# A transformer layer on eight cores: one-row softmax and norm arithmetic, two x buffers in the attention stage, and wider units in the last matmul stage

## The chip, the cores and the metric

One Trainium2 chip; the same program runs on all 8 NeuronCores, two cores to each of the four batch entries, with no exchange between them. Each core has TensorE (PE, matmuls), VectorE (DVE), ScalarE (ACT), GpSimd (POOL), SyncE (SP) and 16 DMA engines. The metric is the device time in microseconds of the slowest core.

## What is computed

```python
# x: (4, 4096, 2048), float32; 16 query heads, 4 key/value heads of 128
def attn(x):                        # x is layer-normalised
    q, k, v = x @ wq, x @ wk, x @ wv          # split into heads
    q, k = rms_norm(rope(q)), rms_norm(rope(k))
    s = q @ k.T / sqrt(128)                   # causal mask, 4 query heads per k/v head
    return softmax(s) @ v @ wo
def ffn(x):                         # w_gate, w_up: (8192, 2048), w_down: (2048, 8192)
    return (silu(x @ w_gate.T) * (x @ w_up.T)) @ w_down.T
x = x + attn(layernorm(x))
x = x + ffn(layernorm(x))
```

## The kernel before

A core owns 2048 of the 4096 positions of one batch entry, as four blocks ("slots") of 512, and works on everything transposed: features on the 128 partitions, positions along the free axis. The program has five phases, each closed by a barrier of all engines.

1. `ph_const` loads small tables: `selb` (a column of ones), `onesr` (a row of ones, bf16), the mask triangle, the bias `kbb` and the scalars `cst`.
2. `ph_kv` normalises x, projects keys and values for all positions into the resident `kT` and `V`.
3. `ph_slots` goes over the four slots. For each: POOL loads the slot's x as bf16 into `xbq` (L668), waiting for the last DVE instruction of the slot before (`q_v`) and its last statistics matmul (`o1_t`); SP loads the cosine and sine tables `csq`, `snq` (L675, L678); PE sums x over the features into `pR` (L683) and DVE makes the negated mean `negmq` (L689). Then come 16 query heads in a small software pipeline: `q_P` projects (L724, rank-one correction L728), `q_R` does the rope on DVE (L740 to L746), `q_S` squares on ACT, sums on PE and makes the reciprocal root on one row with Ln and Exp (L751 to L761), `q_F` splits this row into two bf16 rows `r_hi`, `r_lo` (L768, L770), broadcasts it to 128 partitions by two bf16 matmuls with `onesr` (L301, L303 in `bcast2`) and multiplies (L775). Attention follows for 8 pairs of heads: scores (L816), Exp on ACT (L843), the sums of the probabilities into one row of `pR` (L857) and probabilities times V into `pY` (L864), for 8, 16, 24 or 32 blocks of 128 keys. At the end of a pair DVE takes the reciprocals of the two rows of sums (L885, L887), splits each into two bf16 rows (L888 to L891), PE broadcasts them with four matmuls (L893 to L900), and DVE copies them out of PSUM and scales `pY` into `yT` (L903 to L908). Then the output projection: 16 steps, each with a block of `wo` on POOL (L929), a block of the residual `xr` on SP (L935), 16 matmuls (L947), the addition (L954), a store of the sum to `scr_out1` (L961) and its copy as bf16 into `xbq` (L966). Last the second layernorm: squares on ACT (L975), sums on PE (L981, L985), the rows by `ln_rows` (L280 to L297), two broadcasts into `pS0`, and multiplication and subtraction over the block on DVE (L999, L1004), stored to `scr_ln2` (L1010).
4. `ph_f1` holds the normalised block of all 2048 positions in SBUF and makes silu(gate) times up, 64 steps of 128 matmuls (L1088, L1101), stored as bf16 in `scr_gated`; beside it the down weights are turned into bf16 in `scr_wd`.
5. `ph_f2` is the down projection. A unit is one block of 512 positions and `DSETW` = 4 blocks of 128 output features, so there are 16 units; their results stand in `pDa` and `pDb` in turn. A unit has 8 steps; a step loads 8 x 128 hidden rows of `scr_gated` into `gld` (L1173) and of `scr_wd` into `wdl` (L1178), double buffered, and does 8 x 4 matmuls (L1199). At the end DVE adds the residual `o1t` (loaded on SP, L1157) for each output block into one of two `ost` tiles (L1211), and SP stores it (L1217).

Every DVE and ACT instruction also waits for the one before it on its own engine. The order on each engine is the order of the program text; each DMA queue is served from the engine that issues it, and a DMA that waits holds back what is behind it on that engine.

Of the kernel before, what the change touches and what calls it, by code (L numbers as in the profile page):

```python
# [50 lines left out]
def host_inputs(cfg, x, wq, wk, wv, wo, wg, wu, wd):  # L51
# [15 lines left out]
    for i in range(128):  # L67
        tri[i, :i] = MASK
    shared["selbuf"] = selbuf
    shared["onesrow"] = onesrow  # L70
    shared["tri"] = tri
    consts = np.array([EPS_LN, EPS_RMS, 1.0 / 128.0, -0.5, SCALE,
                       float(np.log(np.float32(SCALE))), 1.0, 0.0],
# [12 lines left out]
    for c in range(2 * B):  # L86
# [10 lines left out]
        kb = np.zeros((128, NIT), np.float32)  # L97
        u = 0
# [81 lines left out]
def build_program(cfg, dump=()):  # L180
# [9 lines left out]
    DSETW = min(4, DK)  # L190
    NDSET = DK // DSETW
    HGS = min(8, HC)
# [4 lines left out]
    for name, shape, dt in [  # L197
# [6 lines left out]
        ("kbias", [128, NIT], F32), ("tri", [128, 128], BF16),  # L204
        ("selbuf", [128, 32], BF16), ("onesrow", [1, 128], BF16),
        ("consts", [128, 8], F32),
# [17 lines left out]
    if "qy" in dump:  # L224
# [6 lines left out]
              "d_const", "d_xk0", "d_xk1", "d_wkv", "d_cs", "d_cs0", "d_cs1", "d_xq",  # L231
# [9 lines left out]
    with es:  # L241
        selb = sb("selb", [128, 32], BF16)
        onesr = sb("onesr", [1, 128], BF16)
        trib = sb("trib", [128, 128], BF16)
        kbb = sb("kbb", [128, NIT])
# [18 lines left out]
        r_hi = asb0("r_hi", [1, 512], BF16)  # L264
        r_lo = asb0("r_lo", [1, 512], BF16)
        m_hi = asb0("m_hi", [1, 512], BF16)
        m_lo = asb0("m_lo", [1, 512], BF16)
# [11 lines left out]
        def ln_rows(ctx, psA, psB, m_stats, eps_idx):  # L279
# [14 lines left out]
            ctx.op("vector", lambda e: e.tensor_copy(r_hi[:, :], row_r[:, :]))  # L294
            ctx.op("vector", lambda e: e.tensor_sub(r_lo[:, :], row_r[:, :], r_hi[:, :]))
            ctx.op("vector", lambda e: e.tensor_copy(m_hi[:, :], row_mr[:, :]))
            ctx.op("vector", lambda e: e.tensor_sub(m_lo[:, :], row_mr[:, :], m_hi[:, :]))  # L297
            return ctx.c("vm")

        def bcast2(ctx, dst, hi, lo, waits):  # L300
            ctx.op("tensor", lambda e: e.matmul(dst, onesr[0:1, :], hi[0:1, :],  # L301
                                                start=True, stop=False), waits=waits)
            ctx.op("tensor", lambda e: e.matmul(dst, onesr[0:1, :], lo[0:1, :],  # L303
                                                start=False, stop=True), inc="tm")
            return ctx.c("tm")

        def ph_const(ctx):
            ctx.op("sync", lambda e: e.dma_start(out=selb[:, :], in_=dram["selbuf"][:, :]), inc="d_const", n=16)
            ctx.op("sync", lambda e: e.dma_start(out=onesr[:, :], in_=dram["onesrow"][:, :]), inc="d_const", n=16)
# [302 lines left out]
        with ExitStack() as at_es:  # L612
# [10 lines left out]
            xbq = asb("xbq", [128, DK * 512], BF16)  # L623
# [3 lines left out]
            reca = asb("reca", [1, 512])  # L627
            recb = asb("recb", [1, 512])
            ra_hi = asb("ra_hi", [1, 512], BF16)
            ra_lo = asb("ra_lo", [1, 512], BF16)  # L630
            rb_hi = asb("rb_hi", [1, 512], BF16)
            rb_lo = asb("rb_lo", [1, 512], BF16)
# [8 lines left out]
            lnt2 = asb("lnt2", [128, (DK // 8) * 512 if DK >= 8 else 512])  # L641
# [4 lines left out]
            xr0 = asb("xr0", [128, 512])  # L646
            xr1 = asb("xr1", [128, 512])
# [13 lines left out]
            def ph_slots(ctx):  # L661
# [3 lines left out]
                      "qcol_s": 0}  # L665
                for slot in range(NS):
                    uslot = sum(ITERS[:slot])
                    ctx.op("gp", lambda e, slot=slot: e.dma_start(  # L668
                        out=A(xbq, 0, [[DK * 512, 128], [512, DK], [1, 512]]),
                        in_=A(dram["xqT"].tensor, slot * 512,  # L670
                              [[OWN, 128], [128 * OWN, DK], [1, 512]])),
                        waits=[("vm", mk["q_v"]), ("tm", mk["o1_t"])],
                        inc="d_xq", n=16)
# [21 lines left out]
                    def q_P(qc):  # L695
# [22 lines left out]
                        for dk in range(DK):  # L718
                            w = []
                            if dk == 0:  # L720
                                w = [(f"d_wq{buf}", m_wq), ("d_xq", m_xq),
                                     ("vm", mq["ropeM"].get(qc - 2, 0)),
                                     ("sm", mq["exp"].get(qc - 2, 0))]
# [522 lines left out]
```

How the kernel before makes its waits and increments, by code:

```python
    def op(self, engine, fn=None, waits=(), inc=None, n=1, guard=True):  # L129
        waits = [(s, v) for (s, v) in waits if v > 0]
        if engine in ("vector", "scalar") and fn is not None:
            gsem = "vm" if engine == "vector" else "sm"
            if guard and self.cnt[gsem] > 0:
                waits.append((gsem, self.cnt[gsem]))
            if inc is None:
                inc = gsem
        if self.cur == engine:
            for s, v in waits:
                self.eng.wait_ge(self.sems[s], v)
            if fn is not None:
                instr = fn(self.eng)
                if inc is not None:
                    instr.then_inc(self.sems[inc], n)
        if fn is not None and inc is not None:
            self.cnt[inc] += n
```

## Time and profile before

| | |
|---|---|
| median of 5 runs | 7091.7 us (7051.29 to 7437.0) |
| the profiled execution | 7094.07 us |
| its span on the slowest core (core 5) | 7092.5 us |
| spans of the 8 cores | 7016.3 to 7092.5 us |
| PE busy | 5254.0 us (74%) |
| DVE, ACT, POOL busy | 1350.8, 1271.3, 350.2 us |

The profile is of one execution, on its slowest core. PE is the matmul engine, PEld its weight loads, which run beside matmuls; a busy PE isn't one at its peak. In the lists of groups, names stand as output<-inputs without buffer numbers, and "idle before" is the time the engine stood still just before such instructions, with what ended it. PEclk is the share of TensorE's full clock that was granted. SPq and POOLq are the queues of SP and POOL in which DMAs are issued.

### The profile page before, as it was taken

The page shows a single profiled execution, that of the slowest core. Times are in us where ns is not written, and L with a number is a line of the kernel's source. Part 1 is how long each engine was busy: PE and PEld are TensorE (multiplying, and loading weights), DVE is VectorE, ACT ScalarE, POOL GpSimd, SP SyncE. Part 2 cuts the span into 40 slices and gives each one's busy share as a digit, 9 for nine tenths or more (in the row PEclk, how much of TensorE's full clock was granted, in tenths as well). Part 3 has the DMA queues.
Part 4 walks back from the last instruction along what each step waited for, and adds up shares of the span by engine and source line. Part 5 has one row for each costly group of instructions (what it writes and reads, how often), then busy time and mean ns, then how long its engine had stood idle before and what let it go on. Part 6 is the DMA issues. An engine that isn't in the chain of part 4 may idle for free. (4 is left out here: it accounts for less than half of the span.)

```text
span 7092.5 us, 57151 instructions; the slowest of 8 cores (7016.3 to 7092.5 us)
## 1 busy us (share of the span) xinstructions
PE 5254.0 (74%) x21360; PEld 1994.4 (28%) x21360; DVE 1350.8 (19%) x1508; ACT 1271.3 (18%) x1307; POOL 350.2 (5%) x342
## 2 busy tenths in 40 slices
PE   5777765557665776478774999999999866766666
PEld 2222221111121111121121444444444322222222
DVE  1222254244315221241211000000000000000000
ACT  1222223113411443136530000000000000000000
POOL 0000010000001000000000101101010000000000
PEclk8777786767777887678886999999999988888888
DMA  4222160552065103530036666666667566666666
GB/s 64 38 30 35 20 63 6 80 67 21 1 88 69 12 1 48 85 36 1 1 48 120 91 101 91 99 95 92 101 91 100 107 214 205 199 208 210 212 213 210
DMA packets 909244, 632.95 MB, mean 89 GB/s; under 512 B 540338, under 2 KB 847538, under 8 KB 908978
## 3 DMA queue, kind: packets, MB, share of 16 engines
q0 software_dynamic: 574752, 205.54, 27.9%
q1 hardware_dynamic: 334226, 423.75, 19.0%
q8 instruction: 180, 2.95, 0.2%
q14 instruction: 86, 0.70, 0.0%
HBM read 725.70 MB, written 109.05 MB: 118 GB/s over the span
## 5 line engine op out<-in xcount | busy, mean ns | idle before, releaser
L1088 PE MATMUL pG<-ln2T,wgb 128*128 128x512 bf16 x4096 | 896.5, 380 | 68.5 <-DMA wub<-wuT 68.5
L1101 PE MATMUL pU<-ln2T,wub 128*128 128x512 bf16 x4096 | 894.5, 379 | 0.0
L843 ACT ACTIVATE probs<-pS,kbb,rsc 128x1024 bf16<-128x1024 f32 (+3 forms) x640 | 729.8, 1140 | 731.0 <-PE pS L816 549.7
L1199 PE MATMUL pDa<-gld,wdl 128*128 128x512 bf16 x2048 | 484.7, 399 | 237.2 <-DMA wdl<-scr_wd 237.1
L1199 PE MATMUL pDb<-gld,wdl 128*128 128x512 bf16 x2048 | 485.4, 400 | 230.2 <-DMA wdl<-scr_wd 230.2
L1088 PEld LDWEIGHTS pG<-ln2T,wgb 128*128 128x128 bf16 x4096 | 401.8, 98 | 553.3 <-issue 72.1
L1101 PEld LDWEIGHTS pU<-ln2T,wub 128*128 128x128 bf16 x4096 | 400.2, 98 | 483.9
L1113 DVE TENSOR_TENSOR gst<-silo,pU 128x2048 bf16<-128x2048 f32 x64 | 146.4, 2288 | 1674.4 <-PE pU L1101 1674.4
L947 PE MATMUL pY<-lyT,wqb 128*128 128x512 bf16 x1024 | 298.0, 463 | 203.2 <-DMA wqb<-wo 176.3
L857 PE MATMUL pR<-probs,selb 128*1 128x512 bf16 (+3 forms) x1280 | 380.3, 380 | 90.4 <-ACT probs L843 48.9
L1110 ACT ACTIVATE silo<-pG 128x2048 f32<-128x2048 f32 x64 | 120.1, 1877 | 1621.0 <-PE pG L1088 1621.0
L816 PE MATMUL pS<-qT,kT 128*128 128x512 bf16 (+3 forms) x1280 | 394.5, 410 | 6.9 <-DVE qT L775 4.5
L864 PE MATMUL pY<-probs,V 128*128 128x512 bf16 (+3 forms) x1280 | 385.8, 385 | 0.0
L724 PE MATMUL pS<-xbq,wqb 128*128 128x512 bf16 x1024 | 315.2, 477 | 62.8 <-ACT rowr L761 30.2
L1199 PEld LDWEIGHTS pDa<-gld,wdl 128*128 128x128 bf16 x2048 | 205.4, 102 | 516.5 <-issue 306.7
L1199 PEld LDWEIGHTS pDb<-gld,wdl 128*128 128x128 bf16 x2048 | 205.7, 102 | 509.9 <-issue 299.8
L496 PE MATMUL ps_V<-wvb,xb 128*128 128x512 bf16 x768 | 227.6, 463 | 157.1 <-ACT V L509 157.1
L893 PE MATMUL pR<-ra_hi,onesr 1*128 1x512 bf16 x32 | 18.5, 579 | 311.0 <-DVE rb_lo L891 311.0
L826 DVE TENSOR_TENSOR pS<-pS,trib 128x256 f32<-128x256 f32 x128 | 55.4, 433 | 923.8 <-PE pS L816 917.4
L947 PEld LDWEIGHTS pY<-lyT,wqb 128*128 128x128 bf16 x1024 | 115.0, 115 | 387.9 <-issue 316.2
L475 PE MATMUL ps_K<-xb,wkb 128*128 128x512 bf16 x768 | 206.0, 430 | 0.0
L816 PEld LDWEIGHTS pS<-qT,kT 128*128 128x128 bf16 x1280 | 118.3, 105 | 249.4 <-issue 188.0
(132 smaller groups left out, 2980.9 us busy)
## 6 DMA issues: line engine op xcount, KB each, us to landing
gld<-scr_gated SPq DMA_DIRECT2D x128, 1024.0 KB, 6.7
wdl<-scr_wd SPq DMA_DIRECT2D x128, 1024.0 KB, 9.7
wqb<-wq POOLq DMA_DIRECT2D x64, 512.0 KB, 6.8
wqb<-wo POOLq DMA_DIRECT2D x64, 512.0 KB, 9.2
wgb<-wgT POOLq DMA_DIRECT2D x64, 512.0 KB, 11.7
wub<-wuT POOLq DMA_DIRECT2D x64, 512.0 KB, 18.3
wds<-wdT POOLq DMA_DIRECT2D x64, 512.0 KB, 19.6
scr_wd<-wds SPq DMA_DIRECT2D x64, 512.0 KB, 13.4
```

The source lines that it names most:

```text
L475: ctx.op("tensor", lambda e, kc=kc, pi=pi, dk=dk, xb=xb: e.matmul(ps_K[:, pi * 512:(pi + 1) * 512], wkb[:, dk * KD + kc * 128: dk * KD + ( ...
L496: ctx.op("tensor", lambda e, ts=ts, dk=dk, xb=xb: e.matmul(ps_V[:, 0:KD], xb[:, dk * 512 + ts * 128: dk * 512 + ts * 128 + 128], wvb[:, dk ...
L724: ctx.op("tensor", lambda e, qc=qc, dk=dk, qp=qp, buf=buf: e.matmul(qp, wqb[buf][:, dk * 128:(dk + 1) * 128], xbq[:, dk * 512:(dk + 1) * 512],
L816: noff=noff, g2=g2: e.matmul(pS[g2][:, h * 512 + noff: (h + 1) * 512], kT[:, kv * KEXT + pos * 128: kv * KEXT + (pos + 1) * 128], qT[:, (h ...
L843: rcol=rcol: e.activation(A(probs[g2], noff, [[1024, 128], [512, 2], [1, 512 - noff]]), A(pS[g2], noff, [[1024, 128], [512, 2], [1, 512 - ...
L857: it=it: e.matmul(pR[0:1, h * 512 + noff:h * 512 + 512], onescol, probs[g2][:, h * 512 + noff:(h + 1) * 512], start=(it == 0), stop=(it == ...
L864: pos=pos, it=it: e.matmul(pY[:, h * 512 + noff:(h + 1) * 512], V[:, pos * KD + kv * 128: pos * KD + (kv + 1) * 128], probs[g2][:, h * 512 ...
L947: ctx.op("tensor", lambda e, dk=dk, yf=yf, pO=pO, buf=buf: e.matmul(pO, wqb[buf][:, yf * 128:(yf + 1) * 128], yT[:, yf * 512:(yf + 1) * 51 ...
L1088: ctx.op("tensor", lambda e, dk=dk, gi=gi, buf=buf: e.matmul(pG[:, gi * 512:(gi + 1) * 512], wgb[buf][:, dk * 128:(dk + 1) * 128], ln2T[:, ...
L1101: ctx.op("tensor", lambda e, dk=dk, gi=gi, buf=buf: e.matmul(pU[:, gi * 512:(gi + 1) * 512], wub[buf][:, dk * 128:(dk + 1) * 128], ln2T[:, ...
L1113: ctx.op("vector", lambda e, buf=buf: e.tensor_mul(gst[buf][:, :], silo[:, :], pU[:, :]), waits=[("tm", m_u), ("sm", mk["silu_s"]), (f"d_g ...
L1199: pD=pD: e.matmul(pD[:, dki * 512:(dki + 1) * 512], wdl[buf][:, hci * DSW + dki * 128: hci * DSW + dki * 128 + 128], gld[buf][:, hci * 512 ...
```

## The change

- At the end of a head pair the reciprocals are made by ACT as Exp(-Ln(sum)), on one row each. The rows stay float32 and are broadcast by one float32 matmul each with a float32 row of ones, `onesrf`. The splitting into two bf16 rows is gone there, in `q_F` and in `ln_rows`; `bcastF` takes the place of `bcast2`.
- `xbq` has two buffers, and the x of the next slot is loaded on POOL once the query heads of this slot are projected. To make room, `xr0`, `xr1` share the memory of `roq0`, `roq1` (so `xr` waits for the last pair's scaling), `reca`, `recb` that of `row_t`, `row_r`; `lnt2` is half as wide, so that the second layernorm squares and applies in pieces half as wide. The bias table is bf16.
- The sums of the next slot wait only for the layernorm's rows (`pRfree`), no longer for its end.
- In `ph_f2` `DSETW` is 8: 8 units of 8 output blocks, all eight PSUM banks in one tile, `pDb` being `pDa`. `o1t` and `wdl` are loaded on POOL, `gld` on SP.

```diff
@@ build_program
-    DSETW = min(4, DK)
+    DSETW = min(8, DK)
     NDSET = DK // DSETW
+    F2ROT = DSETW <= 4
...
@@ ln_rows
             ctx.op("vector", lambda e: e.tensor_mul(row_mr[:, :], row_m[:, :], row_r[:, :]),
                    waits=[("sm", m_rstd)])
-            ctx.op("vector", lambda e: e.tensor_copy(r_hi[:, :], row_r[:, :]))
-            ctx.op("vector", lambda e: e.tensor_sub(r_lo[:, :], row_r[:, :], r_hi[:, :]))
...
-        def bcast2(ctx, dst, hi, lo, waits):
...
+        def bcastF(ctx, dst, row_ap, waits):
+            ctx.op("tensor", lambda e: e.matmul(dst, onesrf[0:1, :], row_ap,
+                                                start=True, stop=True), waits=waits, inc="tm")
+            return ctx.c("tm")
@@ ph_slots
+                def xq_load(slot):
+                    sb2 = slot % 2
+                    ctx.op("gp", lambda e, slot=slot, sb2=sb2: e.dma_start(
+                        out=A(xbqs[sb2], 0, [[DK * 512, 128], [512, DK], [1, 512]]),
...
+                        waits=[("vm", mk["xbq_v"][sb2]), ("tm", mk["xbq_t"][sb2])],
+                        inc=f"d_xq{sb2}", n=16)
+                xq_load(0)
                 for slot in range(NS):
...
-                            waits=([("d_xq", m_xq), ("vm", mk["q_v"])] if dk == 0 else []),
+                            waits=([m_xq0, ("vm", mk["pRfree"])] if dk == 0 else []),
...
                     m_qT = ctx.c("vm")
+                    if slot + 1 < NS:
+                        xq_load(slot + 1)
@@ end of a head pair
-                            ctx.op("vector", lambda e: e.reciprocal(reca[:, :], pR[0:1, 0:512]),
+                            ctx.op("scalar", lambda e: e.activation(reca[:, :], pR[0:1, 0:512],
+                                                                    AF.Ln),
                                    waits=[("tm", m_av)])
...
+                            ctx.op("scalar", lambda e: e.activation(reca[:, :], reca[:, :],
+                                                                    AF.Exp, scale=CC(7, 1)))
...
@@ output projection and second layernorm
-                            waits=[("vm", mk["xres_v"][buf])], inc=f"d_xr{buf}", n=16)
+                            waits=[("vm", max(mk["xres_v"][buf], mk["yev"])),
+                                   (f"d_xr{buf}", ctx.c(f"d_xr{buf}"))], inc=f"d_xr{buf}", n=16)
...
-                    nb = max(1, (DK // 8) * 2)
+                    nb = 2
...
-                    NQB2 = 8 if DK >= 8 else DK
-                    HB2 = DK // NQB2
+                    NQB2 = DK
+                    HB2 = 1
@@ ph_f2
-                    ctx.op("sync", lambda e, gi=gi, dset=dset, ub=ub: e.dma_start(
+                    ctx.op("gp", lambda e, gi=gi, dset=dset, ub=ub: e.dma_start(
                         out=A(o1t[ub], 0, [[DSETW * 512, 128], [512, DSETW], [1, 512]]),
...
-                        waits=[("vm", mk["ep_v"][ub])], inc=f"d_o1{ub}", n=16)
+                        waits=[("vm", mk["ep_v"][ub if F2ROT else 0])], inc=f"d_o1{ub}", n=16)
...
-                    ub = u % 2
+                    ub = (u % 2) if F2ROT else 0
...
-                        ctx.op("sync", lambda e, dset=dset, hg=hg, buf=buf: e.dma_start(
+                        ctx.op("gp", lambda e, dset=dset, hg=hg, buf=buf: e.dma_start(
                             out=A(wdl[buf], 0, [[HGS * DSW, 128], [DSW, HGS], [1, DSW]]),
...
-                            inc=f"d_wl{buf}", n=16)
+                            waits=[("tm", mk["mm_t"][buf])], inc=f"d_wl{buf}", n=16)
```

How the order of the instructions changes, at three places. First the end of a head pair. Before, on DVE, with the semaphores that each waits for (tm, sm and vm count PE, ACT and DVE):

```order
L885 RECIPROCAL reca<-pR 1x512 [waits tm,vm]
L887 RECIPROCAL recb<-pR 1x512 [waits vm]
L888 CAST ra_hi<-reca 1x512 [waits vm]
L889 TENSOR_TENSOR ra_lo<-reca,ra_hi 1x512 [waits vm]
L890 CAST rb_hi<-recb 1x512 [waits vm]
L891 TENSOR_TENSOR rb_lo<-recb,rb_hi 1x512 [waits vm]
L903 COPY roq<-pR 128x512 [waits tm,vm]
```

Now, at the same place on ACT, after the last Exp of the pair; `row_t` and `row_r` are the memory of `reca` and `recb`:

```order
L844 ACTIVATE probs<-pS,kbb,rsc 128x2x128 [waits tm,vm,sm]
L886 ACTIVATE row_t<-pR 1x512 [waits tm,sm]
L889 ACTIVATE row_t<-row_t,cst 1x512 [waits sm]
L891 ACTIVATE row_r<-pR 1x512 [waits sm]
L893 ACTIVATE row_r<-row_r,cst 1x512 [waits sm]
```

Six DVE instructions have become four on ACT; DVE only copies the broadcast rows.

Second, POOL over the slots, in which its DMAs are issued. Before:

```order
L668 DMA xbq<-xqT 128x16x512 [waits tm,sm,vm]
L697 DMA wqb<-wq 128x16x128 x2
L697 DMA wqb<-wq 128x16x128 [waits tm] x14
L929 DMA wqb<-wo 128x16x128 [waits tm] x16
L668 DMA xbq<-xqT 128x16x512 [waits vm,tm]
L697 DMA wqb<-wq 128x16x128 [waits tm] x16
```

Now:

```order
L661 DMA xbq<-xqT 128x16x512 [waits tm,sm,vm]
L698 DMA wqb<-wq 128x16x128 x2
L698 DMA wqb<-wq 128x16x128 [waits tm] x14
L661 DMA xbq<-xqT 128x16x512
L928 DMA wqb<-wo 128x16x128 [waits tm] x16
L698 DMA wqb<-wq 128x16x128 [waits tm] x16
```

The second slot's x has moved ahead of the first slot's `wo` blocks and waits for nothing; the first `wq` blocks of the second slot have no x load ahead of them.

Third, `ph_f2`, at a boundary between units. Before, on SP:

```order
L1217 DMA outT<-ost 128x512 [waits vm] x4
L1157 DMA o1t<-scr_out 128x4x512 [waits vm]
L1173 DMA gld<-scr_gated 128x8x512 [waits tm]
L1178 DMA wdl<-scr_wd 128x8x512
L1173 DMA gld<-scr_gated 128x8x512 [waits tm]
L1178 DMA wdl<-scr_wd 128x8x512
```

Now there are two queues; on POOL, from the start of the stage:

```order
L1161 DMA o1t<-scr_out 128x8x512 [waits tm,sm,vm]
L1161 DMA o1t<-scr_out 128x8x512
L1182 DMA wdl<-scr_wd 128x8x1024 x2
L1182 DMA wdl<-scr_wd 128x8x1024 [waits tm] x6
L1161 DMA o1t<-scr_out 128x8x512 [waits vm]
L1182 DMA wdl<-scr_wd 128x8x1024 [waits tm] x8
```

On SP the stores of a unit's eight results stand ahead of the next unit's `gld`, and on POOL `o1t`, which waits for the last addition of the unit before, stands ahead of the next unit's `wdl`.

## Rows read from the trace of the kernel before

**Rows 1.** The head of the profile's page.

```profile
span 7092.5 us, 57151 instructions; the slowest of 8 cores (7016.3 to 7092.5 us)
```

**Rows 2.** Busy time by stage: slots, F1, F2; the last columns are clock, DMA share, GB/s.

```profile
916.00:3830.00 2914.00, 1882.40 (x6736) 548.21 (x6736) 951.74 (x1188) 947.78 (x937) 150.97 (x132) 0.77 0.31 40
3876.00:5647.00 1771.00, 1770.22 (x8192) 801.98 (x8192) 144.16 (x63) 121.41 (x65) 177.03 (x186) 1.00 0.66 94
5647.00:7092.00 1445.00, 970.10 (x4096) 411.10 (x4096) 46.58 (x65) 0.00 (x0) 0.00 (x0) 0.85 0.68 210
```

**Rows 3.** The waits: engine and line, releaser: us in total, times, longest.

```profile
PE pR L893 <- DVE rb_lo L891: 311.0, 32, 9.7
...
PE pR L683 <- DMA xbq<-xqT: 161.5, 4, 46.6
```

**Rows 4.** What PE sat idle for before the matmuls of L1199 (us, times).

```profile
  DMA wdl<-scr_wd: 467.4, 88
```

**Rows 5.** Timeline at a pair's end: start, us, engine, line; idle and releaser last.

```profile
1097.50 3.35 DVE L885 RECIPROCAL reca<-pR 1x512 f32<-1x512 f32 x1 [1.86 <-PE pY L864]
...
1107.04 0.58 PE L893 MATMUL pR<-ra_hi,onesr 1*128 1x512 bf16 x1 [9.72 <-DVE rb_lo L891]
...
1109.08 0.69 DVE L903 COPY roq<-pR 128x512 f32<-128x512 f32 x1 [2.18 <-PE pR L900]
```

**Rows 6.** Groups by form: count | busy, mean ns of one | idle before.

```profile
L758 ACT ACTIVATE row_t<-pR,cst 1x512 f32<-1x512 f32 x64 | 49.3, 771 | 44.6 <-PE pR L754 44.6
...
L761 ACT ACTIVATE row_r<-row_t,cst 1x512 f32<-1x512 f32 x32 | 23.1, 722 | 3.0
...
L452 PEld LDWEIGHTS ps_rt<-cst,row_r 1*128 1x128 f32 x96 | 21.3, 322 | 39.5 <-issue 39.5
...
L301 PEld LDWEIGHTS pY<-r_hi,onesr 1*128 1x128 bf16 x64 | 5.8, 91 | 31.6 <-issue 31.6
```

**Rows 7.** Timeline at the boundary between the third and the fourth slot.

```profile
2923.50 1.22 DVE L999 TENSOR_TENSOR lnt<-xbq,pS 128x1024 f32<-128x1024 bf16 x1 [1.40 <-PE pS L303]
...
2943.38 1.22 DVE L1004 TENSOR_TENSOR lyT<-lnt,pS 128x1024 bf16<-128x1024 f32 x1
...
2945.21 1.14 POOL L668 DMA_DIRECT2D xbq<-xqT  x1 [68.42 <-DVE lyT L1004]
...
2968.50 5.68 PE L683 MATMUL pR<-xbq,selb 128*1 128x512 bf16 x16 [44.39 <-DMA xbq<-xqT]
...
2978.30 0.68 DVE L740 TENSOR_TENSOR roq<-pS,csq 64x512 f32<-64x512 f32 x1 [3.27 <-PE pS L728]
```

**Rows 8.** Timeline at a boundary between two units of F2.

```profile
5720.97 15.39 PE L1199 MATMUL pDa<-gld,wdl 128*128 128x512 bf16 x64 [3.54 <-DMA wdl<-scr_wd]
...
5736.60 1.49 DVE L1211 TENSOR_TENSOR ost<-pDa,o1t 128x512 f32<-128x512 f32 x2 [87.11 <-PE pDa L1199]
...
5740.60 1.49 DVE L1211 TENSOR_TENSOR ost<-pDa,o1t 128x512 f32<-128x512 f32 x2 [2.52 <-DMA outT<-ost]
5742.59 0.41 SPq L1157 DMA_DIRECT2D o1t<-scr_out  x1
...
5757.08 16.09 PE L1199 MATMUL pDb<-gld,wdl 128*128 128x512 bf16 x64 [20.73 <-DMA wdl<-scr_wd]
```

**Rows 9.** Busy time in two stretches of loading; clock, DMA share, GB/s last.

```profile
20.00:40.00 20.00, 0.08 (x1) 0.08 (x1) 0.00 (x0) 0.00 (x0) 0.00 (x0) 1.00 1.13 164
5743.00:5757.00 14.00, 0.00 (x0) 0.00 (x0) 0.00 (x0) 0.00 (x0) 0.00 (x0) 0.50 0.96 283
```

**Rows 10.** DMA issues: count, KB each, median us from issue to landing.

```profile
wdl<-scr_wd SPq DMA_DIRECT2D x128, 1024.0 KB, 9.7
...
xb<-xkvT POOLq DMA_DIRECT2D x12, 2048.0 KB, 18.0
...
scr_ln<-lyT SPq DMA_DIRECT2D x4, 2048.0 KB, 11.4
...
csq<-cosq SPq DMA_DIRECT2D x4, 128.0 KB, 12.2
```

More of the change, by code:

```diff
@@ L70, in host_inputs @@
     shared["onesrow"] = onesrow
+    shared["onesrf"] = np.ones((1, 128), np.float32)
     shared["tri"] = tri
     consts = np.array([EPS_LN, EPS_RMS, 1.0 / 128.0, -0.5, SCALE,
-                       float(np.log(np.float32(SCALE))), 1.0, 0.0],
+                       float(np.log(np.float32(SCALE))), 1.0, -1.0],
                       np.float32)
@@ new lines, in ph_slots @@
+                            ctx.op("scalar", lambda e: e.activation(recb[:, :], pR[0:1, 512:1024],
+                                                                    AF.Ln))
+                            ctx.op("scalar", lambda e: e.activation(recb[:, :], recb[:, :],
+                                                                    AF.Exp, scale=CC(7, 1)))
+                            m_rec = ctx.c("sm")
+                            ctx.op("tensor", lambda e: e.matmul(pR[:, 0:512], onesrf[0:1, :], reca[0:1, :],
+                                                                start=True, stop=True),
+                                   waits=[("sm", m_rec)])
@@ L902, in ph_slots @@
+                            ctx.op("tensor", lambda e: e.matmul(pR[:, 512:1024], onesrf[0:1, :], recb[0:1, :],
+                                                                start=True, stop=True), inc="tm")
                             m_rb = ctx.c("tm")
                             ctx.op("vector", lambda e: e.tensor_copy(roq0[:, :], pR[:, 0:512]),
-                                   waits=[("tm", m_rb)])
+                                   waits=[("tm", m_rb), ("d_xr0", ctx.c("d_xr0"))])
                             ctx.op("vector", lambda e: e.tensor_copy(tmpq[:, :], pR[:, 512:1024]))
@@ L1140, in build_program @@
             pDa = f2_es.enter_context(nc.psum_tensor("pDa", [128, DSETW * 512], F32))
-            pDb = f2_es.enter_context(nc.psum_tensor("pDb", [128, DSETW * 512], F32))
+            pDb = (f2_es.enter_context(nc.psum_tensor("pDb", [128, DSETW * 512], F32))
+                   if F2ROT else pDa)
             gld = [gld0, gld1]
```

103 lines of the change are left out of this document (40 added, 63 removed).

## The prediction

> **What bounds the kernel now.** I began with the span and its three large stages. The slowest core spans 7092.5 us [rows 1]; the profiled execution took 7094.07 us, 1.6 us more, and the median of the five runs is 7091.7, so a sum made against the profiled execution can be read against the median. By stages [rows 2]: the slots (attention) take 2914 us with PE busy 1882; the first feed-forward stage (F1) 1771 us with PE busy all of it at full clock; the second (F2) 1445 us with PE busy 970 at a mean granted clock of 0.85. F1 is untouched by the edit, so whatever is won or lost lies in the slots and in F2.
>
> Then the waits. In the slots PE stands 311.0 us, 32 times 9.7, before the broadcast of the softmax denominators, for a chain of six DVE instructions, and 161.5 us, 4 times, for the block of x of the next slot [rows 3]. In F2 it stands 467.4 us in 88 waits for wdl [rows 4]. I count 16 of these as long (17.5 to 22.0 us, 322 us together): the first of the stage and one at each of the 15 boundaries between units. The other 72 lie inside units, 145 us in all.
>
> Four changes matter: a shorter chain at the end of a head pair, the early load of x, F2 in 8 units instead of 16, and the small passes of the second layernorm.
>
> **1. End of a head pair (32 times).** Today DVE begins the reciprocals at 1097.50, PE gets its operand at 1107.04 and DVE reads the broadcast at 1109.08 [rows 5]: 9.5 us of rows, then 2.0 us of PE. Now ACT does Ln, Exp, Ln, Exp on one row each, at 771 and 722 ns [rows 6], so 3.0 us, plus three gaps and a hand-over of about 0.1 us each: 3.4 us. That removes 6.1 us. ACT has nothing else then: its next Exp needs the next pair's scores, which stand behind the broadcast on PE. Ln and Exp already follow each other 64 times in the slots with no table load between them, so I charge none.
>
> The broadcast changes from four bf16 matmuls to two float32 ones. No float32 matmul of 512 columns is in the trace. The nearest row is the float32 weight load of 128 columns, 322 ns, against 91 ns for the same load in bf16 [rows 6]: a factor of 3.5. The bf16 matmuls start 0.43 us apart at the half clock, so one float32 matmul is 0.43 us if the type costs nothing and 1.5 us at 3.5 times. Two of them are 0.9 to 3.0 us against 1.7 today; I take the 3.5, the row for the same data type. At the half clock this costs 1.3 us; if PE, idle for 3.7 us instead of 9.7, is still at its full clock, it costs nothing. In F2 a wait of 3.54 us is followed by 64 matmuls in 15.39 us [rows 8] where F1's rate (1771 us for 8192, 0.216 us each) gives 13.8, so part of them ran at half. I therefore lean to the cold price: 6.1 - 1.1 = 5.0 us a pair, **-160 us** (ends: 4.4 and 6.9 us a pair, -140 to -220).
>
> The Trainium skill (FP8 and Floating Point Precision, TensorE Precision Notes) says that true FP32 takes four passes through the array. By that the two matmuls would be 3.4 us at the half clock, 0.4 more than by the row, and this part -150.
>
> The same float32 broadcast serves each query head (64 times) in place of two casts on DVE and two bf16 matmuls. The casts ran beside the square on ACT, so nothing is won; the longer matmul costs 0.32 us at the full clock where DVE is what PE waits for, nothing where PE waits for ACT's Exp anyway. I take **+12 us** (0 to +40).
>
> **2. Slot boundaries (3 times).** DVE ends the layernorm with the row of 2943.38, POOL issues xbq at 2945.21, PE starts its sums at 2968.50, and the first rope of the next slot is at 2978.30 [rows 7]: 33.7 us from end to rope. With two xbq buffers the load runs during attention; PE can do the sums and the first projection while DVE still normalises, and only the mean's row (0.7 us), one matmul and the rope remain. What is late next is the cosine table: its load is still issued when the layernorm ends, on SP behind the 2 MB store of the normalised block. It lands after 12.2 us today and the store after 11.4 [rows 10], both sharing the DMA engines with the xbq load that is gone now; 2 MB at 283 GB/s [rows 9] are 7.4 us, and with both tables behind I take 10 us. So 33.7 becomes 10: -24 each, **-71 us** (ends: 13 us and 2 us, -62 to -95).
>
> **3. The second layernorm (4 times).** Four casts on DVE go (2.6 us), the float32 broadcast adds 0.6 before the first apply and 0.8 before the second. The applies go from 16 of 1.22 us, 1.33 us apart [rows 7], to 32 half as wide; a DVE pass of 512 columns takes 0.69 us [rows 5], with 0.1 between two, so 25.3 us against 21.2. The squares go from 4 wide steps to 8 narrow ones that alternate with PE, +1. Net +4 a slot, **+16 us** (0 to +30). The first residual block xr can no longer be loaded ahead, since it shares roq: +1 a slot, **+4 us**, mostly beside PE's 16 matmuls.
>
> **4. F2.** A unit now has 8 output blocks, so 8 units of 512 matmuls. A step is 64 matmuls, 13.8 us at F1's rate, and needs 1 MB of gld on SP and 2 MB of wdl on POOL, together 3.15 million bytes; it was 2.1 million per 6.9 us. At 283 GB/s [rows 9] that is 11.1 us, and about 2 us of latency makes 13. So the waits inside units nearly vanish: 145 to 10, **-135 us**.
> The half clock after waits goes with them. 4096 matmuls at 0.216 are 885 us; with the 467 of waits that leaves 93 of the 1445, of which I put 13 to the start and end of the stage and 80 to matmuls at half the clock. Eight restarts at 2 us and a few more are 20: **-60 us**.
> The boundaries are fewer and longer. pDb is now pDa, so the next unit may not start before the last add. The adds go in pairs of 1.49 us, the second pair 4.0 us after the first, held by the out stores [rows 8]. Four pairs end at about 13 us instead of 5.5. Only then does POOL issue o1t (2 MB) and wdl, and SP gld. Before wdl has landed 4.2 million bytes go through POOL's queue and up to 2.1 through SP's: 6.3 million at 283 GB/s are 22 us. Before, 14 us did for 3.96 million in just that stretch [rows 8, 9]. 13 + 22 + 2 = 37 us, seven times: 259 against 15 times 20.0 = 300, **-41 us**.
> At the stage's start two o1t loads of 2 MB stand ahead of wdl: +10. The tail has four more adds: +7.
> F2 in all: -135 - 60 - 41 + 17 = **-219 us**.
> That the software queue moves 2 KB pieces as fast as SP's does is the soft point. For it: at the start of the program, with POOL's loads alone, the queue wrote 164 GB/s of bf16 [rows 9], read as twice as much float32. Against it: a 2 MB xb load takes 18.0 us from issue to landing, where wdl on SP took 9.7 for 1 MB [rows 10]. If wdl took those 18.0, a step would be 4 us over, which is +202 on 48 steps. I take the first, since xb reads 4 MB. Range of F2: -20 to -260.
>
> The Trainium skill (DMA: Bandwidth & Descriptors, Issuing engine by pattern) sends simple loads to Sync and calls that path generally faster; this change does the reverse. Its section Issuing engines are not separate DMA queues says all of them run on the same 16 engines and only issue time is saved. By the first rule the second rival below is what to expect, by the latter the forecast.
>
> **Sum.** -160 + 12 - 71 + 16 + 4 - 219 = -418; 7094 - 418 = 6676, and I say **6676 us**.
>
> **Rivals.**
> A. *F2 becomes bound by the software queue.* Steps of 17 instead of 13.8 us, because 2 MB through POOL take near to xb's 18.0. That is 3.2 x 48 = +154, and each boundary (two loads in that queue) +6: in all +196, 6872 us.
> B. *The slots give half.* The float32 broadcast is slower than 3.5 times and the tables hold each slot: 3.2 us a pair is won instead of 5.0, 12 us a slot instead of 24, and each query head pays 0.6: 58 + 36 + 26 = +120, 6796 us. For it: nothing in the trace shows such a matmul.
> C. *Better than forecast.* PE stays at full clock through the pair ends (6.3 us each, -42) and the boundary loads run at 350 GB/s (4 us less, -28): 6606 us.
> D. *Slower than before.* Place: the wait of PE for wdl at each step of F2. If 2 MB on POOL's queue take 18.0 us alone and gld's 1 MB is served beside it (another 3.5), a step is 21.5 us: 7.7 x 48 = +370; two such loads at each boundary +13 x 7, +15 at the start: +476, 7152 us. It decides from a step of 20.5 us on, since each us of step costs 48 plus 14 at the boundaries. Against it: xb reads twice wdl's bytes.
> E. *The change doesn't do what it says:* the early x load waits for a release behind it. The order shows it on POOL ahead of the wo loads with nothing to wait for but the slot before last, so I give this almost nothing: +71, 6747 us.
>
> **How the numbers follow.** Forecast 0.60, A 0.15, B 0.12, C 0.08, D 0.03, E 0.02. 6560 to 6880 holds the forecast with its bounds, A, B, C and E; what is left out is D, an A that is worse than priced and a mixture of A and B. A measurement tells about 1% (71 us) from no change: faster by more 0.95, within 0.02, slower 0.03; only D and something near it come to no gain.
>
> **What would show it.** ACT with four rows between a pair's last matmul and the broadcast, PE's wait there near 3.6 us instead of 9.7; the float32 matmul near 0.75 or 1.5 us. xbq gone from PE's waits in three of four slots, and the table's load as the releaser of the first rope. F2's stretch near 1226 us, 7 waits near 37 us, almost none inside units. I am wrong if PE waits for wdl inside units by more than 3 us a step, or if a boundary is over 45 us, or if the pair's end is not shortened by at least 4 us.

## The result, and the profile after

In some executions of either kernel the cores of one die or of both are granted a lower clock and the time is longer, so all times and ratios below, medians apart, are of executions without that, and the profile of after is read on cores 0 to 3, which had the usual clock in it, mostly on core 1, the slowest of them. Before took 7051 to 7092 us and after 6676.04, 6684.59 and 6704.94 us: a ratio of **0.9452, 95% interval 0.9389 to 0.9516**. Of the 7091.7 us of before that is 6703 us. The forecast of 6676 us is a ratio of 0.941. The medians over all executions are 7330.31 us before (ten) and 6983.38 us after (six); the latter lies above the forecast range of 6560 to 6880 us.

Core 1 after (cores view: span, mean granted clock):

```profile
core 1: 6682.1 us, clock 0.860
```

The same three stages as in [rows 2], slots, F1 and F2:

```profile
916.00:3667.00 2751.00, 1996.75 (x6736) 585.43 (x6736) 597.73 (x916) 1037.07 (x1083) 150.68 (x132) 0.79 0.34 43
3712.00:5484.00 1772.00, 1771.20 (x8192) 802.17 (x8192) 144.14 (x63) 121.43 (x65) 177.03 (x186) 1.00 0.62 94
5484.00:6683.00 1199.00, 903.67 (x4096) 404.03 (x4096) 46.57 (x65) 0.00 (x0) 63.46 (x72) 0.88 0.57 197
```

The slots lose 163 us, F2 246, F1 nothing: about 410 us, all where the prediction looked. DVE's busy time in the slots falls from 952 to 598 us. PE's rises from 1882 to 1997 us; the rows of the broadcasts make up some 80 of these 115 us (140 us in bf16 before, 220 in float32 after).

The waits of PE after (us in total, times, longest), against [rows 3, 4]:

```profile
PE pDa L1203 <- DMA wdl<-scr_wd: 252.6, 10, 37.7
...
PE pR L896 <- ACT row_r L893: 102.1, 32, 3.2
...
PE pS L729 <- DVE negmq L690: 48.9, 3, 16.5
...
PE pDa L1203 <- DMA gld<-scr_gated: 26.5, 1, 26.5
...
PE pR L684 <- DMA xbq<-xqT: 22.2, 1, 22.2
```

At each pair's end PE now waits 3.2 us instead of 9.7. The wait for xbq is there once instead of four times. In F2 the rows for wdl and gld together are 11 waits and 279 us where 88 and 467 stood. The row for negmq is no new loss: those three waits of 16 us are PE, done early with the sums, standing while DVE still normalises, and what follows them is shown below.

A pair's end after, answering to [rows 5]:

```profile
1102.48 0.29 PE L865 MATMUL pY<-probs,V 128*128 128x128 bf16 x2
1102.92 0.59 ACT L886 ACTIVATE row_t<-pR 1x512 f32<-1x512 f32 x1 [0.79 <-PE pY L865]
1103.60 0.72 ACT L889 ACTIVATE row_t<-row_t,cst 1x512 f32<-1x512 f32 x1
1104.41 0.59 ACT L891 ACTIVATE row_r<-pR 1x512 f32<-1x512 f32 x1
1105.09 0.72 ACT L893 ACTIVATE row_r<-row_r,cst 1x512 f32<-1x512 f32 x1
...
1105.96 2.04 PE L896 MATMUL pR<-row_t,onesrf_s 1*128 1x512 f32 x2 [3.19 <-ACT row_r L893]
...
1107.80 1.91 PE L899 MATMUL pR<-row_r,onesrf_s 1*128 1x512 f32 x2
...
1109.63 1.89 PE L817 MATMUL pS<-qT,kT 128*128 128x512 bf16 x4
1109.88 0.69 DVE L902 COPY roq<-pR 128x512 f32<-128x512 f32 x1 [8.80 <-PE pR L899]
```

ACT's four rows stand one behind another (3.0 us from the first to PE's start), then PE needs 3.7 us from 1105.96 to the next scores at 1109.63 for two float32 matmuls, 1.84 us each; the profile shows each as two instructions. The granted clock from 1105.9 to 1109.7 is 0.50, and the bf16 matmuls behind take 0.47 us each: PE is at its half clock. From PE's last matmul to DVE's copy 12.0 us have become 7.4.

The boundary between the third and the fourth slot, answering to [rows 7]:

```profile
2826.17 0.69 DVE L1004 TENSOR_TENSOR lyT<-lnt,pS 128x512 bf16<-128x512 f32 x1
2826.93 0.37 SPq L1010 DMA_DIRECT2D scr_ln<-lyT  x1
...
2827.39 1.96 SPq L676 DMA_DIRECT2D csq<-cosq  x1
2827.90 0.58 PE L729 MATMUL pS<-negmq,qcolsb 1*128 1x512 bf16 x1 [16.25 <-DVE negmq L690]
...
2840.10 0.68 DVE L741 TENSOR_TENSOR roq<-pS,csq 64x512 f32<-64x512 f32 x1 [12.45 <-DMA snq<-sinq]
```

The projection is ready at 2828.5, but the rope stands 12.45 us for the sine table, issued behind the 2 MB store. From the end of the last apply to the rope are 13.2 us where 33.7 were.

The first boundary of F2, answering to [rows 8]:

```profile
5626.63 2.54 PE L1203 MATMUL pDa<-gld,wdl 128*128 128x512 bf16 x11
5629.41 1.49 DVE L1216 TENSOR_TENSOR ost<-pDa,o1t 128x512 f32<-128x512 f32 x2 [142.98 <-PE pDa L1203]
...
5634.16 0.69 DVE L1216 TENSOR_TENSOR ost<-pDa,o1t 128x512 f32<-128x512 f32 x1 [3.26 <-DMA outT<-ost]
...
5645.32 0.69 DVE L1216 TENSOR_TENSOR ost<-pDa,o1t 128x512 f32<-128x512 f32 x1 [0.94 <-DMA outT<-ost]
5646.51 1.10 SPq L1177 DMA_DIRECT2D gld<-scr_gated  x2
5646.55 0.88 POOL L1161 DMA_DIRECT2D o1t<-scr_out  x1 [43.59 <-DVE ost L1216]
5647.43 1.76 POOL L1182 DMA_DIRECT2D wdl<-scr_wd  x2
5666.87 1.44 PE L1203 MATMUL pDa<-gld,wdl 128*128 128x512 bf16 x3 [37.70 <-DMA wdl<-scr_wd]
```

It falls into two halves: 17 us until the last add has gone (5629.2 to 5646.5), the adds after the first two held by the out stores, then 20 us for the loads, none of which is issued before. This is the longest of core 1's first six boundaries: from first to last add they take 13.2 to 16.6 us (14.4 on average); on cores 0, 2 and 3 they take 10.6 to 14.0 us. The DMA issues of core 1 (count, KB each, median us to landing), against 9.7 us for 1 MB on SP [rows 10]:

```profile
wdl<-scr_wd POOLq DMA_DIRECT2D x64, 2048.0 KB, 11.9
```

### The profile page after: what moved, and what is told of

The parts are those of the page before. It is cut to its first block and busy times, and to the rows that moved or that the text cites. A ratio compares the mean times of both kernels' runs of the same rounds, so it can differ in the third digit from the quotient of the medians.

```text
span 6814.2 us, 56736 instructions; the slowest of 8 cores (6644.6 to 6814.2 us)
## 1 busy us (share of the span) xinstructions
PE 5464.8 (80%) x21360; PEld 2061.8 (30%) x21360; DVE 996.9 (15%) x1236; ACT 1358.0 (20%) x1451; POOL 413.2 (6%) x414
## 5 line engine op out<-in xcount | busy, mean ns | idle before, releaser
L1203 PE MATMUL pDa<-gld,wdl 128*128 128x512 bf16 x4096 | 1052.2, 429 | 253.3 <-DMA wdl<-scr_wd 229.2
L1203 PEld LDWEIGHTS pDa<-gld,wdl 128*128 128x128 bf16 x4096 | 439.1, 107 | 866.3 <-issue 770.0
L725 PE MATMUL pS<-xbq,wqb 128*128 128x512 bf16 x1024 | 321.7, 484 | 41.7 <-ACT row_r L763 20.4
L1216 DVE TENSOR_TENSOR ost<-pDa,o1t 128x512 f32<-128x512 f32 x64 | 44.3, 692 | 1270.1 <-PE pDa L1203 1216.3
L725 PEld LDWEIGHTS pS<-xbq,wqb 128*128 128x128 bf16 x1024 | 117.2, 119 | 254.0 <-issue 198.8
L928 POOL DMA_DIRECT2D wqb<-wo x64 | 73.1, 1141 | 1852.0 <-PE pY L947 1785.9
## 6 DMA issues: line engine op xcount, KB each, us to landing
scr_wd<-wds SPq DMA_DIRECT2D x64, 512.0 KB, 10.6
```

What stands on the lines that cost most here:

```text
L725: ctx.op("tensor", lambda e, qc=qc, dk=dk, qp=qp, buf=buf: e.matmul(qp, wqb[buf][:, dk * 128:(dk + 1) * 128], xbq[:, dk * 512:(dk + 1) * 512],
L1203: pD=pD: e.matmul(pD[:, dki * 512:(dki + 1) * 512], wdl[buf][:, hci * DSW + dki * 128: hci * DSW + dki * 128 + 128], gld[buf][:, hci * 512 ...
```

## Experiments

There are nine. After took 6684 us (the middle of its three), before 7053 to 7116 us beside these runs. e3, e4, e5, e6 and e9 rest on one execution each, so a difference of some 20 us in their whole time (after's own three spread over 29) is weak; what is read from marks inside the traces is firmer.

**e1, F2's edits alone on the kernel before.**

```diff
-    DSETW = min(4, DK)
+    DSETW = min(8, DK)
...
-            pDb = f2_es.enter_context(nc.psum_tensor("pDb", ...))
+            pDb = (f2_es.enter_context(...) if F2ROT else pDa)
...
-                        ctx.op("sync", ... wdl[buf] ...
+                        ctx.op("gp", ... wdl[buf] ...
```

> The kernel before with the new ph_f2 alone (8 units of 8 output blocks, o1t and wdl on POOL). Theory 1 (the forecast's mechanism: the gain of F2 is its own and comes from fewer steps' waits, and the slots' gain is separate): F2 takes 1199 us as in the changed kernel against 1445, the slots stay at 2914, so 7092 - 246 = 6846 us, ratio 0.965. Theory 2 (the F2 gain leans on something in the slots, or the two gains overlap): F2 above 1230 us, ratio above 0.97.

Measured: 6837.36 and 6845.66 us, with 8 long waits of 265 us and 0.3 us of short ones in F2, as in after. F2's part is worth 228 us by itself against the two runs of before beside it (7052.77 and 7085.35) and 250 against 7091.7; what is left to after's 6684, some 158 us, is the slots' part, near to the 163 that the slots' stretch lost.

**e2, o1t and wdl on SP's queue**, after otherwise.

```diff
-                    ctx.op("gp", ... o1t[ub] ...
+                    ctx.op("sync", ... o1t[ub] ...
...
-                        ctx.op("gp", ... wdl[buf] ...
+                        ctx.op("sync", ... wdl[buf] ...
```

> The changed kernel with o1t and wdl issued on SP again, DSETW still 8. Theory 1 (the width is what counts: all queues feed the same 16 DMA engines and 3 MB per step fit into 13.8 us either way): F2 stays within 15 us of 1199, boundaries within 3 us of 35.6 (both loads still stand behind the last add), so 6684 us plus or minus 15. Theory 2 (the second queue is what counts, since on one queue wdl lands behind gld): steps take 15 to 16 us, 48 x 1.5 = +70 us, near 6755 us. Theory 3 (the software queue is the slower one, as its 18 us for xb suggested): SP is faster, boundaries 32 us, -25 us, near 6660 us.

Measured: 6653.27, 6657.66 and 6668.21 us, 27 us less than after. The wait of PE, and then the issue, on core 1:

```profile
PE pDa L1203 <- DMA wdl<-scr_wd: 240.8, 8, 31.8
```

```profile
wdl<-scr_wd SPq DMA_DIRECT2D x64, 2048.0 KB, 10.8
```

Inside units nothing changes, since a step of 13.8 us hides either queue's load, and the loads themselves don't differ by queue: the median time of a wdl load to landing is 11.2 to 11.9 us on cores 0 to 3 of after and 10.8 to 12.7 us on those here. At the first six boundaries the wait on core 1 is 31.2 us on average and was 36.2. 2 us of these 5 lie in the adds, which differ as much from core to core; on all eight cores the stretch from the last add to PE's start is 17.9 to 18.6 us and was 20.7 to 21.4, so about 3 us are real. They don't show a slower queue, for with the queue the order changed. In after two gld blocks on SP run beside POOL's loads, and the second (1 MB, not needed yet) has landed within 0.2 to 0.7 us of wdl; here it stands behind wdl and lands 2.7 to 3.6 us after it. In after 6.3 million bytes are through when PE starts, here 5.2: some 300 and 290 GB/s. So the 3 us go with what stands ahead of the first wdl; a run with the second gld held back and wdl left on POOL would prove it and wasn't made. The Trainium skill (DMA: Bandwidth & Descriptors, Issuing engine by pattern) sends simple loads to Sync. The whole kernel is 27 us shorter so, but no run here shows that the path itself is faster. The Trainium skill (the same page, Issuing engines are not separate DMA queues) says that starting DMAs on several engines saves issue time only. The landing times inside units agree.

**e3, the reciprocals back on DVE**, the float32 broadcast kept.

```diff
-                            ctx.op("scalar", lambda e: e.activation(reca[:, :], pR[0:1, 0:512],
-                                                                    AF.Ln),
...
-                            m_rec = ctx.c("sm")
+                            ctx.op("vector", lambda e: e.reciprocal(reca[:, :], pR[0:1, 0:512]),
+                                   waits=[("tm", m_av)])
+                            ctx.op("vector", lambda e: e.reciprocal(recb[:, :], pR[0:1, 512:1024]))
+                            m_rec = ctx.c("vm")
```

> The changed kernel with the two reciprocals of a pair on DVE again (no cast, float32 broadcast kept). Theory 1 (the row arithmetic is on the path one for one): the chain ahead of the broadcast is 2 x 3.35 + gaps = 7.0 us instead of 3.2, so +3.8 us a pair, 32 x 3.8 = +122, slots 164 shorter become 42 shorter, near 6806 us. Theory 2 (the pair's gain came from the casts and from PE's clock, not from the reciprocals): less than +60 us.

Measured: 6807.38 us, theory 1's number. The intervals between pair ends grow by 3.8 us a pair, and PE's wait shows it:

```profile
1103.95 3.35 DVE L886 RECIPROCAL row_t<-pR 1x512 f32<-1x512 f32 x1 [1.86 <-PE pY L865]
1107.40 3.35 DVE L888 RECIPROCAL row_r<-pR 1x512 f32<-1x512 f32 x1
...
1110.89 2.04 PE L890 MATMUL pR<-row_t,onesrf_s 1*128 1x512 f32 x2 [7.12 <-DVE row_r L888]
```

PE's wait is 7.1 us against 3.2. Moving the two reciprocals to ACT is worth 3.8 us a pair, 122 us in all, most of the 143 that the pair ends gained; four casts less and a dearer broadcast nearly cancel.

**e9, a bf16 row broadcast at the pair's end**, so two bf16 matmuls in place of two float32 ones. This rounds each reciprocal to bf16.

```diff
-  ctx.op("scalar", lambda e: e.activation(reca[:, :], reca[:, :], AF.Exp, ...
+  ctx.op("scalar", lambda e: e.activation(recab[:, :], reca[:, :], AF.Exp, ...
-  ctx.op("tensor", lambda e: e.matmul(pR[:, 0:512], onesrf[0:1, :], reca[0:1, :],
+  ctx.op("tensor", lambda e: e.matmul(pR[:, 0:512], onesb[0:1, :], recab[0:1, :],
```

(the same for recb)

> The changed kernel with each reciprocal row written by ACT as one bf16 row and broadcast by one bf16 matmul (the reciprocals are rounded to bf16, which the changed kernel doesn't do). It measures the float32 broadcast. Theory 1 (two float32 matmuls of 512 columns take 3.8 us at the half clock against 0.9 in bf16, all of it on the path): 2.9 us a pair less, -93 us, near 6591 us. Theory 2 (a part is hidden: PE's clock comes back later when it has been idle, and the scores behind the broadcast then take longer): -50 us or less.

Measured: 6614.22 us, 70 less than after. A pair's end:

```profile
1111.56 0.58 PE L900 MATMUL pR<-negmq,onesb_s 1*128 1x512 bf16 x1 [3.19 <-ACT xsq L897]
1111.94 0.63 PE L903 MATMUL pR<-xsq,onesb_s 1*128 1x512 bf16 x1
1112.74 0.69 DVE L906 COPY roq<-pR 128x512 f32<-128x512 f32 x1 [6.05 <-PE pR L903]
```

From the start of the first broadcast to DVE's copy: 1.2 us, against 3.9 with float32, 2.7 us less. The intervals between pair ends shrink by 2.9 us on every core, 94 us in 32, as theory 1 said. The total shows 70, for it is that of core 5, whose output projections took 497 us in this run where the eight cores average 485. Against the four bf16 matmuls of before, about 2.0 us [rows 5], the float32 broadcast gives back 1.9 us a pair: the largest loss inside the slots.

**e4, the load of x at its old place and under its old wait**, with two buffers kept.

```diff
-                xq_load(0)
                 for slot in range(NS):
+                    xq_load(slot)
...
-                    if slot + 1 < NS:
-                        xq_load(slot + 1)
```

> The changed kernel with the x of each slot loaded at the slot's start again, behind the layernorm's last DVE instruction (the rest as changed). Theory 1 (the early load carries the whole of the slot boundary's gain): from the last apply to the next rope 34 to 37 us again instead of 14.4, three times +21 = +63 us, near 6747 us. Theory 2 (the table's load would hold the rope in any case, so the x load matters little): under +25 us.

Measured: 6723.12 us, 39 more than after, between the two theories. The wait is back:

```profile
PE pR L684 <- DMA xbq<-xqT: 164.6, 4, 48.1
```

From the last apply to the first rope the three boundaries are 33 to 34 us again, 20 more each: the 60 us that were expected. But the output projections are 15 us shorter, and that is not chance. The last of their 16 additions, in after and then here, on core 1:

```profile
1398.77 1.14 POOL L698 DMA_DIRECT2D wqb<-wq  x1 [11.97 <-PE pY L947]
1407.94 0.69 DVE L954 TENSOR_TENSOR o1f<-pY,roq 128x512 f32<-128x512 f32 x1 [8.65 <-DMA roq<-xqT]
```

```profile
1400.60 0.69 DVE L952 TENSOR_TENSOR o1f<-pY,roq 128x512 f32<-128x512 f32 x1 [3.77 <-DMA roq<-xqT]
```

In after POOL is free to load two `wq` blocks for the next slot's query heads beside the last residual block, and the last addition comes 8.8 us behind the one before it (mean of the first three slots, all cores). Here, as in before, POOL is held by x until the layernorm has ended, and it comes after 4.6 us (before 4.7). In the fourth slot, which has no next, it is 4.5 us in after too, and all kernels with the early load show 8.6 to 9.1 us in the first three. So the early load has a price of 4.2 us a slot, 13 in all, that the sum didn't have. The query heads are another 5 us shorter here.

**e5, the tables loaded with x, during attention.**

```diff
+                def cs_load(slot, m):
+                    ctx.op("sync", lambda e, slot=slot: e.dma_start(
+                        out=csq[:, :], in_=A(dram["cosq"].tensor, slot * 512, [[OWN, 64], [1, 512]])),
+                        waits=[("vm", m)], inc="d_cs", n=16)
...
+                cs_load(0, 0)
...
                         xq_load(slot + 1)
+                        cs_load(slot + 1, m_qT)
```

> The changed kernel with the next slot's cosine and sine tables loaded right after the last query head, not at the slot's end. Theory 1 (the tables are what holds the first rope of a slot, as the forecast's term of 10 us said; 13.1 to 13.9 us measured): mean's row to rope falls from 13.5 to about 4 (PE then needs one rank-one matmul and DVE its turn), three times -10 = -30 us, near 6654 us. Theory 2 (the rope is held by PE or by the store ahead of it in the DMA engines, and the tables only land at the same time): under -8 us.

Measured: 6662.37 us, 22 less. The same boundary:

```profile
2818.34 0.69 DVE L1007 TENSOR_TENSOR lyT<-lnt,pS 128x512 bf16<-128x512 f32 x1
...
2820.97 0.68 DVE L743 TENSOR_TENSOR roq<-pS,csq 64x512 f32<-64x512 f32 x1 [1.15 <-PE pS L731]
```

1.9 us from the end of the last apply to the rope, released by PE: the tables were the last wait ahead of the rope, 11 us of it. The total gains 22 of these 34 us. The waits of PE on this core show where the rest stays:

```profile
PE pS L727 <- DMA wqb<-wq: 12.1, 3, 5.7
```

After has no such row for its projections (L725). The third block of `wq` is loaded only when PE has used the first, and the tables' wait had hidden that load: once per boundary 4 us of the gain come back. The load of `wq` is what is late next.

**e6, the next unit's first loads issued before this unit's adds**, as each buffer of gld and wdl comes free, and o1t inside the unit.

```diff
                         mk["mm_t"][buf] = ctx.c("tm")
+                        if hg + 2 < NHG:
+                            fm[hg + 2] = f2_load(hg + 2)
+                        elif u + 1 < len(units):
+                            ngi, ndset = units[u + 1]
+                            nfm[hg + 2 - NHG] = f2_load(hg + 2 - NHG, ngi, ndset)
```

> The changed kernel with the first two loads of the next unit put ahead of the adds and stores in the program text, and o1t loaded inside the unit before. Theory 1 (a boundary is 17 us of adds and stores plus some 18 us of loads in a row, in series only by their order): boundaries fall from 35.6 to about 18, the stage's start from 32 to 17, F2 from 1199 to about 1060, near 6545 us. Theory 2 (the loads are bound by the DMA engines at the boundary, which the out stores also need): the adds get slower as the loads run, boundaries 25 us or more, above 6600 us.

Measured: 6592.86 us, 92 less than after, but not what was expected. The waits of PE in F2:

```profile
PE pDa L1204 <- DVE ost L1223: 147.4, 7, 21.5
PE pDa L1204 <- DMA wdl<-scr_wd: 22.5, 2, 22.1
```

The waits for loads at the boundaries are gone (a boundary is 21 us, by theory 1 18), and the full 21 us of the adds stand in their place. The adds themselves have become slower: on core 3 they took 10.6 to 12.3 us at the first six boundaries of after, on all its cores 10.6 to 16.6, here 18.1 to 23.6. They wait for out stores, and these now share the DMA engines with the early loads, as theory 2 said. After's own last boundary, the only one there with a load beside the adds, shows the same: 18.4 us on core 1.

**e8, e6 and e5 with four output tiles, and each PSUM bank released by its own add.**

```diff
+            ost2 = gsb("ost2", [128, 512])
+            ost3 = gsb("ost3", [128, 512])
...
-                        buf = dki % 2
+                        buf = dki % 4
...
+                                if hg == 0 and hci == 0:
+                                    w = (w if dki == 0 else []) + [("vm", bank_v[dki])]
```

> The two edits before together, plus four ost tiles instead of two and a wait of each output block's first matmul for its own block's add only. Theory 1 (what is left of a boundary is the pace of adds held by their stores): boundaries fall to 2 to 8 us, F2 to about 960, the slots by 30 us, near 6430 us, ratio 0.91. Theory 2 (the adds are held by the stores' bandwidth, not by the number of tiles): boundaries stay above 12 us, above 6480 us.

Measured: 6515.50 and 6518.02 us. 12 us are left at each boundary: the first four adds run back to back, the other four each behind a store, 86 us of waits behind adds in all. This is short of the 6430 us of theory 1, by the adds' second half, and in the range of theory 2 (stores' bandwidth). e10 decides between the two. What the tiles and what the release by bank give, 53 us together beyond e5 and e6, was not tried apart.

**e10, the same with eight output tiles.**

> The kernel of e8_best (tables early, loads of the next unit ahead of its adds, a wait for each bank) with eight output tiles in the second half of the feed-forward in place of four. In e8_best the profile shows, at each of the seven boundaries, four adds back to back (0.77 us apart) and the other four each behind a store (idle before them 4.19, 1.33, 1.38 and 1.26 us, ended by outT<-ost), and the matmuls wait 12.9 us in sum (90.1 us in all for seven), one wait behind each add. Theory (the stores pace the adds because a tile must be stored before it is filled again): with eight tiles all eight adds run back to back; the matmuls wait 1.84 us and seven times 0.42 us, about 4.8 us a boundary, 8.1 us less, 57 us in all, and the time is about 6459 us (6516 less 57). Rival (the boundary is bound by the traffic: the stores and the loads of the next unit share the DMA engines and matmuls then wait for wdl instead): the waits behind the adds go and come back behind wdl, and the time stays above 6495 us.

Measured: 6439.78, 6452.01 and 6462.18 us, ratio to before **0.9098, interval 0.9038 to 0.9159**. Waits in F2, and a boundary:

```profile
PE pDa L1217 <- DMA wdl<-scr_wd: 26.1, 8, 20.6
PE pDa L1217 <- DVE ost L1236: 21.9, 51, 1.9
```

```profile
5609.09 6.26 DVE L1236 TENSOR_TENSOR ost<-pDa,o1t 128x512 f32<-128x512 f32 x8 [131.55 <-PE pDa L1217]
...
5610.07 0.38 PE L1217 MATMUL pDa<-gld,wdl 128*128 128x512 bf16 x1 [1.22 <-DVE ost L1236]
```

The eight adds run in one row of 6.26 us and PE follows them bank by bank, with 3.0 to 4.3 us of waits at a boundary. The 64 us against e8 are those of the stores (57 expected); no wait for loads took their place (outside the stage's start, 5.5 us for wdl in all). So the number of tiles held the adds. This kernel beats before by 9.0% where the change as made gives 5.5%.

## Why the prediction was right and wrong

The step that failed is the first one: **"so a sum made against the profiled execution can be read against the median"**. The medians of before then and now, 7091.7 and 7330.31 us for the same kernel, show that it did not hold. Nor is the measured 6983.38 us a time of any execution: it is the middle between 6784.44 and 7182.32 us, the third and fourth of six that run from 6676 to 7331. The five times behind the 7091.7 already ran from 7051 to 7437 us, but the range had bounds for every cost of the kernel and none for the executions that the median is taken over. That the change is worth what it was said to be is not touched by this: the ratio of the two medians is 0.953, near the 0.9452 above. The sum itself was made against one execution of 7094 us, and beside such executions it came out: 6676 forecast, 6676 to 6705 measured. Term by term, from the same marks in both traces (before on core 5, after on core 1):

| term | forecast | measured | by |
|---|---|---|---|
| end of a head pair, 32 | -160 | -143 | 28 intervals between DVE copies, 1310.1 to 1184.9 us, 4.47 each |
| query head's broadcast | +12 | +4 | from rope to first copy, less its four pair ends |
| slot boundaries, 3 | -71 | -64 | start of the last apply to first rope, 107.3 to 43.0 us |
| second layernorm, 4 | +16 | +28 | last add to last apply, 199.6 to 227.3 us |
| xr | +4 | +11 | the adds of the output projection, 468.7 to 479.3 us |
| F2 | -219 | -247 | end of F1's matmuls to the end, 1445.6 to 1198.2 us |
| sum | -418 | -411 | 7092.5 to 6682.1 us is -410 |

That the sums agree to 7 us is in part luck: errors of up to 28 us cancel, and the two cores are the slowest of different dies. On cores 0 to 3 in both traces the terms are -144, +14, -62, +31, +8 and -213, together -366 us, and the ratio above means -389. The mechanisms are the same either way; how well single terms were met is not.

- **Pair end.** The mechanism held (ACT's rows 3.0 us with the gaps inside the 3.4 priced, PE at its half clock, no table load between Ln and Exp). PE's wait fell by 6.5 us for the 6.1 priced, and the broadcast costs 1.9 us more for the 1.1 priced. Mis-sized was "one float32 matmul is 0.43 us if the type costs nothing and 1.5 us at 3.5 times": it is 1.84 us, 4.3 times the 0.43. The weight load was the nearest row and still not near enough. By the four passes that the Trainium skill states (FP8 and Floating Point Precision, TensorE Precision Notes) the prediction's estimate for the part came to -150, closer to the -143 than the row's -160; the measured 4.3 times agrees roughly.
- **Query heads.** One float32 broadcast stands with 1.12 us in the profile at the full clock, and a part is hidden where PE stands for ACT, as said. The +4 comes from the choice of cores: core 5's query heads were the longest of the eight before. Cores 0 to 3 give +14 for the 12 priced.
- **Slot boundary.** The tables were late next, as forecast; 13.2 us and not 10. e5 shows what stood behind them: a block of `wq`, with 4 us.
- **Second layernorm.** Two terms were too small: the applies went up by 5.2 us a slot (21.1 to 26.3) for the 4.1 priced, and the eight narrow steps of squares by 2 to 5 for the 1 priced. That such narrow passes are what costs is read from the marks; it was not tried alone.
- **xr.** The row is not xr's. e4 keeps xr as changed, and its output projections take 470 us on average over the eight cores, as in before (472) and e1 (473), where the eight kernels with the early load of x have 479 to 485: it is the price of that load that e4 shows, through the `wq` blocks that POOL is free to load.
- **F2.** Waits inside units 145 to 3 (forecast 10). Boundaries 300 to 244 (forecast 259): the first six 36.2 on average for the 37 forecast, some 14.4 in the adds and 21.4 in the loads where I had 13 and 24. The last is only 26.5: there is no o1t load ahead of wdl there, so the next unit's first wdl had landed 2.9 us before the first add began and the second landed 11.4 us after it, while the adds ran; only gld stood behind the stores. The half clock and the stage's ends give the remaining -58 for my -53, and the start costs 10 more, as forecast.
- **Rivals.** A, which the passage on the skill's first rule calls the second, fell: wdl landed after 11.9 us, not 18, steps inside units did not wait, and e2 finds no slower load on POOL. B's first half (a slower float32 matmul) is true in kind, at 0.5 us a pair. C did not come, PE was at half clock at the pair ends. D and E show in no row.

So more than half of F2's gain (142 of 247) came from steps long enough to hide their loads, and the price was paid at boundaries made serial: adds, then loads. PSUM holds a single set, and POOL's first load, o1t, waits for the last add and holds wdl behind it; the last boundary, without it, is 10 us shorter. e6, e8 and e10 give that price back without touching the tiling.

## What to carry to other kernels

When a tile is doubled so that all of PSUM is one accumulation set, the loads of the next unit have to be issued before the epilogue, each bank should be released by itself, and the staging tiles should cover the whole epilogue; together that was worth some 210 us more here (232 to e10, less the 22 of e5). When a load is moved ahead in a queue, look at what it had been holding back: here the loads behind it moved up beside one that was needed sooner, for 13 us. A row that is broadcast through TensorE should be priced by its type: two float32 matmuls of 512 columns cost 2.7 to 2.9 us more than two bf16 ones at the half clock, where the whole pair end gained 4.5. A sum made for one execution is to be set beside the spread of executions before a range is put on a median.

## What the runs showed of the hardware

- A float32 matmul with one row and 512 columns stands in the profile as two instructions and takes 1.84 us at the half clock, 4.3 times a bf16 one.
- ACT takes 0.59 us for a row of 512 straight from PSUM (Ln) and 0.72 us for the Exp behind it; DVE's reciprocal of the same row is 3.35 us.
- A 2 MB load beside one of 1 MB lands after 11.2 to 11.9 us on POOL's queue and 10.8 to 12.7 on SP's, from core to core. A load of 1 MB that isn't needed yet, served beside the others at a boundary, goes with 3 us more until PE starts.
- Out stores of 256 KB through two tiles pace eight adds to 10.6 to 16.6 us, and to 18.1 to 23.6 beside the next unit's loads; with a tile for each add it is 6.3 us.
